# Softmax totals by VectorE sums and a 16-column fp32 matmul, and 48 loop slots written out

## The reference, cut to what matters

```python
q = layernorm(x) @ Wq            # 32 heads of 128, in 8 groups of 4
k, v = ctx @ Wk, ctx @ Wv        # 8 heads of 128
q, k = rope(q), rope(k)
logits = 30 * tanh((q k^T) * 0.0884 / 30), masked
weights = softmax(logits)        # over the 128 keys
x = x + tanh(g_xattn) * (weights v) @ Wo
x = x + tanh(g_ffn) * ffn(layernorm(x))   # 4-bit weights, 1376 wide, silu gate
```

## Time and profile before

| what | value |
|---|---|
| median of 3 runs | 818.39 us (818.18 to 819.52) |
| profiled execution, its time | 819.66 us |
| profiled execution, its span | 817.6 us |
| TensorE busy | 782.9 us, 96% of the span |
| VectorE busy | 586.8 us, 72% |
| GpSimd busy | 493.0 us, 60% |
| ScalarE busy | 352.5 us, 43% |
| mean granted TensorE clock | 0.987 of full speed |

### The profile page before, as it was taken

One profiled execution on the slowest core, in us unless ns is written; L12 is line 12 of the kernel. 1 busy time (PEld: TensorE's weight loads), 2 busy tenths in 40 slices (PEclk: granted clock), 3 DMA queues, 4 the chain that ended last, 5 costly groups with the idle time before them and its releaser, 6 DMA issues.

```text
span 817.6 us, 12509 instructions
## 1 busy us (share of the span) xinstructions
PE 782.9 (96%) x3905; PEld 652.1 (80%) x3905; DVE 586.8 (72%) x1224; ACT 352.5 (43%) x715; POOL 493.0 (60%) x392
## 2 busy tenths in 40 slices
PE   4789999999999999999999999999998689999998
PEld 3667888888888888888888888888887468888786
DVE  7797777777777777777777777776787577787531
ACT  3554444444344343443443444434444345555420
POOL 3689765566556666556665566556886466566400
PEclk9999999999999999999999999999999799999999
DMA  8410302010210201020102101120020134442011
GB/s 288 132 53 17 113 1 79 1 52 1 78 52 0 77 0 51 0 77 0 51 6 71 51 0 48 29 47 1 3 59 1 36 75 103 103 112 48 0 65 38
DMA packets 56970, 41.29 MB, mean 51 GB/s; under 512 B 22922, under 2 KB 44298, under 8 KB 56938
## 3 DMA queue, kind: packets, MB, share of 16 engines
q1 hardware_dynamic: 56938, 40.90, 17.1%
HBM read 38.77 MB, written 2.11 MB: 50 GB/s over the span
## 4 chain that ended last, share of the span: by engine, by line
PE 89%; DVE 6%; POOL 3%; issue 1%; ACT 1%; DMA 0%; DVEq 0%; POOLq 0%
PE ps_o L53 7%; PE ps_o L55 7%; PE ps_o L54 7%; PE bank_q L55 7%; PE bank_q L54 7%; PE bank_q L53 7%; PE ps_qT L1121 3%; PE bank_kv L54 3%; PE bank_kv L55 3%; PE bank_kv L53 3%; PE ps_s L54 3%; PE ps_s L53 3%; PE ps_s L55 3%; PE ps_pv L53 2%; PE ps_pv L55 2%; PE ps_pv L54 2%
## 5 line engine op out<-in xcount | busy, mean ns | idle before, releaser
L511 POOL TENSOR_TENSOR aT_lo<-attn,aT_hi 128x512 fp32r<-128x512 f32 x64 | 96.6, 1510 | 167.8 <-ACT aT_hi L678 167.8
L638 ACT CAST qT_hi<-ps_qT 128x512 fp32r<-128x512 f32 x64 | 37.5, 585 | 170.3 <-PE bank_kv L1122 91.1
L53 PE MATMUL bank_q<-wq_hi,xT_hi 128*128 128x512 f32 x256 | 107.6, 420 | 1.6 <-DVE wq_lo L806 1.6
L53 PE MATMUL ps_o<-wo_hi,aT_hi 128*128 128x512 f32 x256 | 100.3, 392 | 2.3 <-POOL aT_lo L511 1.6
L55 PE MATMUL bank_q<-wq_hi,xT_lo 128*128 128x512 f32 x256 | 102.2, 399 | 0.0
L54 PE MATMUL bank_q<-wq_lo,xT_hi 128*128 128x512 f32 x256 | 102.1, 399 | 0.0
L55 PE MATMUL ps_o<-wo_hi,aT_lo 128*128 128x512 f32 x256 | 99.9, 390 | 0.0
L54 PE MATMUL ps_o<-wo_lo,aT_hi 128*128 128x512 f32 x256 | 99.6, 389 | 0.0
L496 POOL TENSOR_TENSOR probs<-probs,keepT 128x512 f32<-128x512 f32 x64 | 83.2, 1300 | 13.0 <-ACT probs L654 13.0
L524 POOL TENSOR_TENSOR roped<-q_cos,q_sin 128x512 f32<-128x512 f32 x61 | 79.0, 1295 | 1.8 <-DVE q_sin L827 1.7
L898 DVE TENSOR_TENSOR qT_lo<-ps_qT,qT_hi 128x512 fp32r<-128x512 f32 x64 | 44.3, 692 | 42.7 <-ACT kT_hi L639 42.7
(11 more groups left out here) (220 smaller groups left out, 2199.7 us busy)
## 6 DMA issues: line engine op xcount, KB each, us to landing
wo_raw<-in_Wo SPq DMA_DIRECT2D x8, 1024.0 KB, 5.0
wq_raw<-in_Wq SPq DMA_DIRECT2D x7, 1024.0 KB, 5.7
packed<-in_gate_q SPq DMA_DIRECT2D x40, 64.0 KB, 2.3
packed<-in_up_q SPq DMA_DIRECT2D x40, 64.0 KB, 2.3
packed<-in_down_q SPq DMA_DIRECT2D x10, 256.0 KB, 3.4
acc<-in_x SPq DMA_DIRECT2D x8, 256.0 KB, 8.2
cT_raw<-in_ctx SPq DMA_DIRECT2D x8, 256.0 KB, 8.3
wkv_raw<-in_Wk SPq DMA_DIRECT2D x8, 256.0 KB, 5.9
```

The lines of the kernel that those rows point to most:

```text
L53: nc.tensor.matmul(out, w_hi, m_hi, start=first, stop=False)
L511: nc.gpsimd.tensor_tensor(aT_lo[:], attn[:], aT_hi[:].bitcast(F32), ALU.subtract).then_inc(a_split, 1)
L638: nc.scalar.copy(qT_hi[:], ps_qT[:])
```

## The change

Three things. The totals: VectorE transposes probs itself in 32x32 blocks (into r_tot) and sums each block's 32 values, which leaves 16 partial sums per partition (partial); one fp32 matmul of 16 moving columns with the matrix fold completes them over the four blocks of partitions, and the reciprocal reads its result from PSUM directly. The two ones matmuls and the transpose of ps_tot go. TensorE gets a wait on the partial sums before the new matmul; the new VectorE operations stand ahead of the rotary products of q; ScalarE's exp gets a wait on the transpose of two slots before. The set-up: fold is built from the identity by two VectorE operations, in place of GpSimd's memset of ones. The loop: the 48 middle slots are written out on every engine.

```diff
--- before.py
+++ after.py
@@ -158,7 +158,8 @@
         seen = sb("seen", [P, 1], F32)
         live = sb("live", [P, 1], F32)
         dead = sb("dead", [P, 1], F32)
-        ones = sb("ones", [P, P], F32R)
+        fold = sb("fold", [P, P], F32)
+        partial = sb("partial", [P, GC // 32], F32)
         r_tot = sb("r_tot", [P, GC], F32)
         r_small = sb("r_small", [P, GC // 32], F32)
 
@@ -221,7 +222,7 @@
         ld_ctx = [sem(f"ld_ctx{b}") for b in range(B)]
         ld_tab, ld_mask, ld_gates = sem("ld_tab"), sem("ld_mask"), sem("ld_gates")
         ld_wq, ld_wkv, ld_wo = sem("ld_wq"), sem("ld_wkv"), sem("ld_wo")
-        id_zero, id_done, ones_done, half_done = sem("id_zero"), sem("id_done"), sem("ones_done"), sem("half_done")
+        id_zero, id_done, half_done = sem("id_zero"), sem("id_done"), sem("half_done")
         stats_done, moments_done, var_done = sem("stats_done"), sem("moments_done"), sem("var_done")
         rstd_done, xn_done = sem("rstd_done"), sem("xn_done")
         x_T, x_hi, x_lo = sem("x_T"), sem("x_hi"), sem("x_lo")
@@ -238,7 +239,7 @@
         s_done, tanh_done, exp_done, masked = sem("s_done"), sem("tanh_done"), sem("exp_done"), sem("masked")
         p_rounded, p_split, pv_done = sem("p_rounded"), sem("p_split"), sem("pv_done")
         tot_done, inverted, norm_done = sem("tot_done"), sem("inverted"), sem("norm_done")
-        tot_turned, r_spread = sem("tot_turned"), sem("r_spread")
+        p_turned, p_summed, r_spread, fold_done = sem("p_turned"), sem("p_summed"), sem("r_spread"), sem("fold_done")
         a_rounded, a_split, o_done, acc_done = sem("a_rounded"), sem("a_split"), sem("o_done"), sem("acc_done")
 
         share_scaled = sem("share_scaled")
@@ -277,9 +278,9 @@
 
             for s in range(B):
                 slot(0, 0, s)
-            with eng.Fori(0, (SLOTS - 2 * B) // LOOPED) as i:
-                for s in range(B, B + LOOPED):
-                    slot(i * LOOPED, i * (LOOPED // B), s)
+            for s in range(B, SLOTS - B):
+                base = (s - B) // LOOPED * LOOPED
+                slot(base, base // B, s - base)
             for s in range(SLOTS - B, SLOTS + 3):
                 slot(0, 0, s)
 
@@ -409,7 +410,6 @@
                 pool.wait_ge(id_zero, 1)
                 nc.gpsimd.affine_select(out=ident[:], in_=ident[:], compare_op=ALU.not_equal, fill=1.0,
                                         base=0, pattern=[[-1, P]], channel_multiplier=1).then_inc(id_done, 1)
-                nc.gpsimd.memset(ones[:].bitcast(F32), 1.0).then_inc(ones_done, 1)
                 nc.gpsimd.memset(zero_words[:], 0).then_inc(words_clear, 1)
                 pool.wait_ge(half_done, 1)
 
@@ -650,6 +650,7 @@
                     nc.scalar.activation(capped[:], ps_s[:], ACT.Tanh, scale=ATTN_MULT / MAX_ATTN).then_inc(tanh_done, 1)
                     wait(act, tanh_done, j + 1)
                     wait(act, p_split, j - 1)
+                    wait(act, p_turned, j - 1)
 
                     nc.scalar.activation(probs[:, s % 2, :], capped[:], ACT.Exp,
                                          scale=MAX_ATTN).then_inc(exp_done, 1)
@@ -811,6 +812,11 @@
                 norm_moments(1)
                 norm_apply(1)
                 norm_moments(2)
+                dve.wait_ge(id_done, 1)
+                nc.vector.reduce_sum(r_tot[:, 0:32], ident[:].rearrange("p (i c) -> p c i", i=4), AX_X).then_inc(fold_done, 1)
+                dve.wait_ge(fold_done, 1)
+                nc.vector.tensor_copy(fold[:].rearrange("p (i c) -> p i c", i=4),
+                                      r_tot[:, 0:32].unsqueeze(1).to_broadcast([P, 4, 32])).then_inc(fold_done, 1)
                 dve.wait_ge(keep_T, 1)
                 nc.vector.tensor_copy(keepT[:], ps_pv[:, 0:T]).then_inc(tab_done, 1)
                 dve.wait_ge(mask_step, 6)
@@ -916,6 +922,13 @@
                         wait(dve, p_rounded, j - 1)
                         nc.vector.tensor_tensor(p_lo[:], probs[:, par, :], p_hi[:].bitcast(F32),
                                                 ALU.subtract).then_inc(p_split, 1)
+                    if runs(s - 2):
+                        wait(dve, masked, j - 1)
+                        wait(dve, norm_done, j - 2)
+                        nc.vector.transpose(r_tot[:], probs[:, (s - 2) % 2, :]).then_inc(p_turned, 1)
+                        wait(dve, p_turned, j - 1)
+                        wait(dve, tot_done, j - 2)
+                        nc.vector.reduce_sum(partial[:], r_tot[:].rearrange("p (c e) -> p c e", e=32), AX_X).then_inc(p_summed, 1)
                     if runs(s):
                         wait(dve, q_done, j + 1)
                         wait(dve, q_roped, j)
@@ -944,9 +957,7 @@
                     if runs(s - 2):
                         wait(dve, tot_done, j - 1)
                         wait(dve, norm_done, j - 2)
-                        nc.vector.transpose(r_tot[:], ps_tot[:]).then_inc(tot_turned, 1)
-                        wait(dve, tot_turned, j - 1)
-                        nc.vector.reciprocal(r_small[:], r_tot[:].rearrange("p (c e) -> p c e", e=32)[:, :, 0]).then_inc(inverted, 1)
+                        nc.vector.reciprocal(r_small[:], ps_tot[:, 0:GC // 32]).then_inc(inverted, 1)
                         wait(dve, inverted, j - 1)
                         nc.vector.transpose(r_tot[:].rearrange("p (c e) -> p c e", e=32),
                                             r_small[:].unsqueeze(2).to_broadcast([P, GC // 32, 32])).then_inc(r_spread, 1)
@@ -1109,7 +1120,6 @@
                             mm.then_inc(down_done, 1)
                     return mm
 
-                pe.wait_ge(ones_done, 1)
 
                 def transpose_qk(j, s):
 
@@ -1169,8 +1179,10 @@
                         wait(pe, norm_done, j - 2)
                         if s == 2:
                             pe.wait_ge(tab_done, 1)
-                        nc.tensor.matmul(ps_tot[:], ones[:], p_hi[:], start=True, stop=False)
-                        nc.tensor.matmul(ps_tot[:], ones[:], p_lo[:], start=False, stop=True).then_inc(tot_done, 1)
+                        wait(pe, p_summed, j - 1)
+                        if s == 2:
+                            pe.wait_ge(fold_done, 2)
+                        nc.tensor.matmul(ps_tot[:, 0:GC // 32], fold[:], partial[:], start=True, stop=True).then_inc(tot_done, 1)
                         mm = split_matmul(nc, ps_pv[:], v_hi[:, vb, :], v_lo[:, vb, :], p_hi[:], p_lo[:], True, True)
                         mm.then_inc(pv_done, 1)
                     if s == TAIL + 9:
```

## The result

The changed kernel takes **811.92 us**, median of 4 runs (811.05 to 812.60), against 818.71 us for the kernel before, measured beside it: ratio 0.9912, 95% interval 0.9898 to 0.9925. The time falls by 6.8 us where 11.3 were forecast; the forecast of 807.1 us was 4.8 us too low and the time lies inside the range. The profiled execution took 811.05 us, 809.3 of them span.

The account below looks back on a forecast made before the run. TensorE was taken to bound the middle slots: 58 x 0.247 = 14.3 us gained, less 1.3 at the first and 1.7 at the last slots, 11.3 us off 818.39, giving 807.1 us; range 799.5 to 817.

Parts of the forecast that it names:

- TensorE sets the slot and VectorE follows: Middle slots: TensorE alone sets the pace; VectorE's added 0.75 us per slot fits in its gaps, over 2 us in all.
- X: TensorE's price per slot for the new 16-column fp32 matmul: 0.22 us taken, between 0.11 and 0.44.
- The row that the prediction named as deciding: TensorE, end of last ps_s step to start of pv: 0.22 us instead of 0.46, to decide between the rivals.
- rival B: Totals on TensorE: the small matmul is nearly hidden, X at 0.11 or less, 800.7 us; chance 0.11.
- First slots: VectorE-bound slots 2 to 4 and building fold: a loss of 1.3 us, from 0 to 3.
- Last slots: Slots 63 to 65, where transpose and sum delay TensorE: a loss of 1.7 us, between 0.5 and 3.
- Writing the 48 slots out: Middle slots, loop edge: worth 0, since the edge costs TensorE nothing that can be got back.
- C: Between ps_s and pv: the fp32 matmul eats the gain, 819.8 us at a price of 0.44; chance 0.09.
- D: VectorE's transpose and sum, slowed by GpSimd, bring the totals late: slots 0.95 us longer, 876 us; chance 0.03.
- E: Middle slots: writing them out starves an engine of instructions, 821.5 us at 0.3 us per slot; chance 0.02.
- The signs of being wrong: fp32 matmul over 0.4 us, a wait on the sum in the middle slots, or ends costing over 5 us.

Follow-up runs that it names:

- e6: Changed kernel with a second, unused sum of the transposed probabilities on VectorE in slots 6 to 57: 812.32 us, ratio 0.9911 to the kernel before.
- e3: Changed kernel with fold and partial held as fp32r instead of fp32: 803.38 us, ratio 0.9812 to the kernel before.
- e5: Changed kernel with the totals' fp32 matmul issued twice in slots 6 to 57: 824.22 us, ratio 1.0055 to the kernel before.
- e9: Changed kernel with the old totals from slot 60 on, the rest new: 807.92 us, ratio 0.9865 to the kernel before.
- e8: Changed kernel with the old totals in the first four slots, the rest new: 809.55 us, ratio 0.9881 to the kernel before.
- e1: Changed kernel with the 48 middle slots kept as a loop, so only the totals are new: 816.3 us, ratio 0.9975 to the kernel before.
- e4: Changed kernel with the old totals in the first four slots and from slot 60 on: 805.83 us, ratio 0.9847 to the kernel before.
- e10: New totals with the loop kept, plus waits at VectorE's start that move its loop body by 20 places: 816.18 us, ratio 0.9965 to the kernel before.

## Why the prediction was right in sign and 4.8 us too low

- **TensorE sets the slot and VectorE follows: right.** No wait on the sum in the middle slots, 1.1 us of slack where 1.0 was worked out, sum 0.69 and transpose 0.70 undisturbed by GpSimd, the gap before q_cos gone. e6 shows it by experiment. Only the gap before acc was forecast near 0.8 and is 1.08.
- **X, two steps of 0.11: borne out, size a little off.** Two records are there, and one matmul in fp32 costs twice what it costs in fp32r (0.24 to 0.247 against 0.114; e3, e5). That each step is a weight load and not some other fixed cost is argued: no run changed the number of columns. 0.22 was taken, 0.247 measured: over 57 slots 1.5 us less. With 57 slots in place of 58 another 0.2. The row that the prediction named as deciding was badly chosen: between the end of ps_s and the start of pv stand 0.13 us where 0.22 was forecast, which alone would have spoken for rival B; the rest of the price is on pv's own row. The Trainium skill's page "FP8 and Floating Point Precision", section "TensorE Precision Notes", speaks of four passes for true fp32; a full step of 0.11 for each would have been 0.44, and neither the records (two) nor the price (0.24) bears that out for 16 columns.
- **First slots, 1.3: the number about right, partly by luck.** 1.44 by the slots' starts, and 0.14 ahead of them. Of the 1.3, 0.4 was for building fold, and that was wrong: its two operations take 0.60 us on VectorE, but q's roped of slot 0 behind them takes 1.14 instead of 1.69, and TensorE's transposes of slot 0 start only 0.14 later than before. The walk through the queues gave 0.9 where 1.44 came. TensorE's waits there did not grow by 1 us either. The one ahead of the totals grew (1.87 instead of 0.33), others shrank (roped 0.81 instead of 1.67), and from 40.0 to 46.6 us the granted clock was 0.50, that is 1.2 GHz, where it had stayed at 1.00 after waits of 0.33 and 1.67 in the kernel before. How much of the 1.44 is the clock is not separated.
- **Last slots, 1.7: the term that was furthest off.** They cost 3.9 (1.54 + 2.36), which e9 confirms with 4.0 given back by the medians and 3.85 by its trace. The wait in slot 64 came as forecast (2.47 us, "2 to 3"). What was missed has three parts. In slot 63 the forecast had TensorE's transposes 0.7 us later than before, and they come 1.54 later: q_cos is pushed by 2.3 us and not by 1.4, because xn ahead of it takes 1.62 instead of 0.67; in e3's trace, where xn takes 0.57, that slot loses 0.83 (7.88 us instead of 7.05). By the totals' matmul of slot 64 the changed kernel is 3.24 us behind, where 2.7 was worked out. Then 1.0 of it was taken to come back, and nothing does: in e8's trace, with the clock at 1.00, 3.32 is still missing at the first gate matmul, with a second wait of 1.82 in slot 65. And 0.6 is TensorE's clock, which fell in the changed kernel's trace and was in no term. 0.5 + 1.0 + 0.6 is, to 0.1, the 2.2 us.
- **Writing the 48 slots out, 0: right for the kernel before, wrong for the one after.** The step was read from the earlier trace rows, the edge of the old loop, and applied to the new one. The new totals lengthen VectorE's body past what stays loaded, and at the same time they put 1.4 us between p_lo and TensorE. Without the writing out the change would have given 2.1 us (e1). It cost the forecast nothing, because the change makes both edits; as a reading of what does the work it was wrong.
- **Rivals.** B (X at 0.11) is what the fp32r form gives, C and D did not occur, and E is the opposite of what the runs show: the written-out slots starve nothing, the loop does.
- **The signs of being wrong.** Two of the three did not come: X is under 0.4 us, and no wait on the sum stands in the middle slots. The third did: the ends were to cost at most 5 us, and they cost 1.4 + 3.9 = 5.3 by the slots' starts and 6.1 by e4. The range, up to 817 us, was wide enough to hold that.

The sum: 14.3 - 1.7 (X and slot count) = 12.6; less 1.4, 3.9 and 0.14 ahead of the first slot = about 7.1 at the end of attention; 6.8 by the medians.

## What to carry to other kernels

A matmul's price is read from the start before it to the start of the second one behind it: a short one puts nearly half of its cost or more on its neighbour's row. When an edit lengthens a loop's body, read the loop's edge again, and look for instruction packets inside a pass and for idle time with "issue" as its releaser; an edge that was free is free only for that length and that slack. And a long wait of TensorE at a phase's end can cost more than its own length: read the granted clock of the stretch behind it, in more than one trace. Where the two ends of a pipeline are bound by another engine than its middle, keep the old form there (6.1 us here).

## What the runs showed of the hardware

- A VectorE loop body of 358 instructions stays loaded over three passes; one of 406 is fetched again in each (three 8-KB packets from 260 to 380 us, 26 or 27 in the queue against 16) and leaves VectorE idle for 2.2 to 2.8 us at each edge, with the new totals (in two positions) as with mere waits added.
- TensorE's granted clock was low behind some waits: 0.50 for 6.6 us from the wait of 1.87 on and 0.55 for 3.7 us behind that of 2.47 (the changed kernel), 0.68 and 0.54 to 0.66 over 3.6 us behind waits of 1.64 and 1.65 (second edge of e1, both edges of e10). It was 1.00 behind waits of 0.81 and 1.67 (before), of 1.65 (first edge of e1), of 2.43 (e8) and of 2.47 (e3). So waits of the same length went both ways, near 1.65 and near 2.45; where it fell at a loop edge the next slot lost 1.7 us, and at the end of the slots 0.56. It may be part of why single executions of one kernel lie 1 to 2 us apart; that was not followed up.
- A 16-column fp32 matmul with 128x128 weights takes 0.24 us of TensorE's time, the fp32r form 0.114.
- p_lo on VectorE stretches from 0.68 to between 1.22 and 1.79 us where GpSimd works all the while beside it, while the transpose and the sum keep 0.70 and 0.69 in the same traces, also where GpSimd works beside them.
